# Two exponentials given ahead of two feed-forward blocks, and a router task moved from tap 84 to tap 80

## The chip, the cores and the metric

The kernel runs on one core of a Trainium2 chip. Times are device microseconds of that core. The kernel before has a median of 1639.95 us over 3 runs (1638.41 to 1640.2).

## The reference, cut to what matters

The input is 8 images of 256 channels by 32 x 32 positions, in float32. Each image goes through a linear-attention block and a mixture of six feed-forward experts, both with a residual.

```python
x = x + conv_attention(layernorm_over_channels(x))
t = tokens(x)
t = t + ffn(layernorm(t))

def ffn(x):
    logits = x.mean(axis=1) @ router_w.T
    probs = softmax(logits)
    vals, idx = top_k(probs, 2)
    vals = vals / vals.sum()
    ew = einsum(vals, partition_table[idx])
    ew = where(ew > 1e-6, ew, 0)
    h = gelu(x @ W1[e] + b1[e])
    out_e = h @ W2[e] + b2[e]
    return sum over e of ew[e] * out_e
```

The expert weights `ew` of an image depend on the mean over its tokens. There is one set of six weights per image; all experts are computed for all images. The attention block holds a 1 x 1 convolution to 768 channels (q, k and v), a depthwise 5 x 5 convolution of these, a grouped 1 x 1 convolution (the aggregation) and linear attention with 8 channels per head.

## The kernel before, in words

An image is kept as two tiles of 128 channels by 1024 positions. The layers with large matmuls split float32 values into a high and a low float16 part and add three products.

The order of all work is one list, `ORDER`, that `schedule()` (lines 81 to 269) writes. Every engine walks through this list and issues its own share of each item, in the order of the list. An engine waits by semaphores only, so what stands behind a waiting instruction on its engine waits too. Round `j` of the list works on the attention of image `j`, closes the attention of image `j - 1` (called `new`) and fills the room between with feed-forward blocks. A block (`ffn`) is 128 hidden units of 512 tokens; an image has 32 of them (two halves of the tokens, 16 blocks each).

`fill(k)` (lines 113 to 123) gives up to `k` blocks. With each it gives three things: the block's own first-layer matmuls and gelu (`ffn`); the expert-weight scaling and the splitting of earlier blocks whose image has its exponentials given (`gsplit`); and the second-layer matmuls (`second`) of the block four places back. Blocks 0 and 1 of an image may be given before its exponentials are given (line 115), its scalings may not (line 118). Behind the last block of a half a `final` evicts the sum.

The items around the change, with what each engine does:

- `logits`: two matmuls on TensorE (line 649), and an eviction of 11 numbers on ScalarE (line 818).
- the max task on VectorE (`max_task`, lines 1018 to 1026), which finds the largest logits and gives their negative as a bias.
- `exp` on ScalarE (lines 753 to 757): two small exponentials, of all logits and of the two largest. They need the max task. Exponential and gelu need different function tables, so a table load stands ahead of each when the other was last.
- the router task on VectorE (`route_task` and `ew_task`, lines 1028 to 1065): 14 small instructions in a chain. They need both exponentials. The last one writes `ewg`, the expert weights times a scale.
- `ffn`: six matmuls (line 533) into one of two PSUM banks `wbk`, and a gelu on ScalarE (line 825), which frees the bank.
- `gsplit`: two scalings on ScalarE (lines 730 and 731) that read `ewg`, and a subtraction on GpSimd (line 960).
- `second`: six matmuls (line 546) into the accumulator `acc`. The first block of a half waits until `final` has evicted the half before (line 544; the eviction is line 764).
- `agg`: the aggregation, four pieces of matmuls (line 584) for `k`, each into a bank `wbk` and evicted by ScalarE (line 790).
- `squares` on ScalarE (line 744), `sums` on GpSimd (lines 867 and 869), `stats` on TensorE (line 635), `rnorm` on GpSimd (line 883) and `rbc` on TensorE (line 644), evicted by ScalarE (line 816): the normalisation of a later image.
- `base`: some taps of the depthwise convolution of the next image, scaled on ScalarE (lines 700 and 705) and added on GpSimd (lines 924 and 930).

The two banks `wbk` are shared by all matmuls but `second`: a piece may start when the piece two places before it in the list has been evicted (lines 560 to 562).

VectorE does the other taps of the depthwise convolution, line 1113 for the most part, 138 instructions an image in three pairs of tiles (132 for image 0). Its small tasks are placed by their count of taps: the table `OF_LAST` (line 1077) puts tasks of the image before ahead of a given tap of this image. With 46 taps to a pair, taps 76 to 91 belong to the second pair. Behind the last image no taps are left, and the tasks follow each other.

Of the kernel before, what the change touches and what calls it, by code (L numbers as in the profile page):

```python
# [64 lines left out]
def base_taps(s, m):  # L65

    return (0 if m in (2, 3) else len(BASE_TAPS)) if s == 0 else 3
# [8 lines left out]
def tap_ops(s):  # L76

    return [(pair, tap, m) for pair in PAIRS for tap in tap_order(s, pair) for m in (2 * pair, 2 * pair + 1)]


def schedule():

    o = []
    given = set()
    waiting = []
    stream = [(s, f) for s in range(B) for f in range(NCH * FT)]
    todo = list(stream)
    unsplit = []

    def give(*items, n=1):  # L90
        for it in items:
            o.append(it)
            given.add(it)
            if it[0] in BANKED and n > 1:
                base(n)

    def base(n):
        o.extend(waiting[:n])
        del waiting[:n]

    def rest():
        base(len(waiting))

    def add_base(s, a):
        waiting.extend(("base", s, m, i) for m in (a, a + 1) for i in range(base_taps(s, m)))

    def second(k):
        s, n = stream[k]
        give(("second", s, n))
        if n % FT == FT - 1:  # L110
            give(("final", s, n // FT))

    def fill(k):
        for _ in range(k):
            if todo and ("low", todo[0][0], 1, CT - 1) in given and (("exp", todo[0][0]) in given or todo[0][1] < 2):
                i = len(stream) - len(todo)
                give(("ffn",) + todo.pop(0))
                while unsplit and ("exp", unsplit[0][0]) in given:
                    give(("gsplit",) + unsplit.pop(0))
                unsplit.append(stream[i])  # L120
                if i >= LAG:
                    second(i - LAG)
            base(1)

    def left(s):
        return sum(it[0] == s for it in todo)

    def qkv(s, m):
        return [("qkv", s, m, ch) for ch in range(NCH)]

    def agg(s, m):
        return [("agg", s, m, ch) for ch in range(NCH)]

    def norm_in(s):

        return [[("squares", s, 0, 0)], [("squares", s, 0, 1), ("sums", s, 0)],
                [], [("stats", s, 0), ("rnorm", s, 0)], [], [],
                [("rbc", s, 0, 0), ("rbc", s, 0, 1)], [("apply", s, 0, 0)], [("apply", s, 0, 1)]]

    def norm_out(s):  # L140

        return [[("high", s, 0, 0)], [("low", s, 0, 0), ("high", s, 0, 1)], [("low", s, 0, 1)]]

    give(("squares", 0, 0, 0), ("squares", 0, 0, 1), ("sums", 0, 0), ("weights", 0), ("stats", 0, 0), ("rnorm", 0, 0), ("rbc", 0, 0, 0), ("rbc", 0, 0, 1), ("apply", 0, 0, 0),
         ("apply", 0, 0, 1), ("weights", 1), ("high", 0, 0, 0), ("low", 0, 0, 0), ("high", 0, 0, 1), ("low", 0, 0, 1))
    give(*[it for m in range(2, QT) for it in qkv(0, m)])
    add_base(0, 2)
    add_base(0, 4)

    for j in range(B + 1):  # L150
        d, c, a, f = j < B, j >= 1, j + 1 < B, j + 2 < B
        new, nxt = j - 1, j + 1
        n = 3 if j == 0 else 1
        if c:
            give(*agg(new, 0), *agg(new, 1))
            fill(1)
            for t in range(TT):
                give(("att", new, 1, t))
                if t in (2, 5):
                    fill(1)  # L160
                if t == 3:
                    give(("scale", new, 1, 0))
            give(("scale", new, 1, 1))
        if j == 0:
            for group in norm_in(1)[:2]:
                give(*group)
        if d:
            give(*qkv(j, 0), *qkv(j, 1), n=n)
            add_base(j, 0)
            if j == 0:  # L170
                for group in norm_in(1)[2:]:
                    give(*group, n=n)
        out = norm_out(nxt) if a else [[], [], []]
        toks = [("tok", j, t) for t in range(TT)] if d else []
        if c:
            fill(1)
            give(("back", new, 1, 0, 0), ("back", new, 1, 0, 1))
            fill(1)
            give(("back", new, 1, 1, 0), ("back", new, 1, 1, 1))
            fill(1)  # L180
            give(("proj", new, 0, 0), *out[0], *toks[:2])
            give(("proj", new, 0, 1), *toks[2:4])
            give(("proj", new, 1, 0), *out[1], *toks[4:6])
            give(("proj", new, 1, 1), *toks[6:])
        else:
            give(*out[0], *out[1])
        if c:
            give(*out[2])
            fill(1 if d else 2)
            give(("squares", new, 1, 0), ("squares", new, 1, 1), ("sums", new, 1))  # L190
        else:
            give(*out[2], *toks, n=n)
        if d:
            give(("relu_q", j, 0))
            give(("kv", j, 0, 0), ("kv", j, 0, 1), n=n)
            give(("mask", j, 0), ("relu_q", j, 1))
        if c:
            fill(1)
            give(("stats", new, 1), ("rnorm", new, 1))
            fill(1)  # L200
        if d:
            give(*[("att", j, 0, t) for t in range(4)], n=n)
        if c:
            fill(1 if d else 2)
            give(("rbc", new, 1, 0), ("rbc", new, 1, 1), ("apply", new, 1, 0), ("apply", new, 1, 1))
        if d:
            give(("scale", j, 0, 0))
            give(*[("att", j, 0, t) for t in range(4, TT)], n=n)
        if c:
            give(("high", new, 1, 0))  # L210
            fill(1 if d else 2)
            give(("high", new, 1, 1))
        if d:
            give(("scale", j, 0, 1))
        if c:
            give(("low", new, 1, 0), ("low", new, 1, 1))
            if a:
                give(*qkv(nxt, 2))
        if d:
            give(*[("back", j, 0, ch, g) for ch in range(NCH) for g in range(2)], n=n)  # L220
        if c:
            give(("logits", new))
            if a:
                give(*qkv(nxt, 3))
            else:
                fill(1)
            fill(left(new - 1) + 2)
            give(("exp", new))
        rest() if j == 0 else None
        if d:  # L230
            give(*agg(j, 2), *agg(j, 3))
            if a and c:
                add_base(nxt, 2)
        if j == 0:
            give(*qkv(1, 2), *qkv(1, 3))
            add_base(1, 2)
        if d:
            for group in norm_in(j + 2) if f else [[]] * 5:
                give(*group)
                fill(1)  # L240
            fill(1)
            give(*agg(j, 4))
            fill(1)
            give(*agg(j, 5))
            fill(1)
            if a:
                for m in (4, 5):
                    for it in qkv(nxt, m):
                        give(it)
                        fill(1)  # L250
                add_base(nxt, 4)
            else:
                fill(4)
            give(("kv", j, 1, 0))
            fill(2)
            give(("kv", j, 1, 1))
            fill(1)
            give(("mask", j, 1))
            while left(new) > KEEP and new >= 0:
                fill(1)  # L260
            if j == 0:
                rest()
    k = len(stream)
    fill(k)
    rest()
    give(("gsplit",) + stream[-1])
    for i in range(k - LAG, k):
        second(i)
    return o
# [46 lines left out]
def build(nc, x, w_qkv, w_dw, w_pw, w_proj, bn, bn_rows, w_router, w1, b1, w2, b2, parts, out):  # L316
    with ExitStack() as ctx:
# [3 lines left out]
        def sem(name):  # L321
            return ctx.enter_context(nc.semaphore(name))
# [109 lines left out]
        route = sem("route")  # L432
# [532 lines left out]
        def _(dve):  # L965
# [108 lines left out]
                    ew_task(s, s % 2)  # L1074


            OF_LAST = {16: ("rden", 1, 0), 21: ("rden", 1, 1), 76: ("max",), 84: ("route",)}
            OF_THIS = {62: ("rden", 0, 0), 68: ("rden", 0, 1)}
            OF_FIRST = {92: ("rden", 0, 0), 98: ("rden", 0, 1)}

            for s in range(B + 1):
                if s == B:
                    for n in sorted(OF_LAST):
                        small_task(OF_LAST[n], s - 1)
                    continue
                for n, (pair, tap, m) in enumerate(tap_ops(s)):
                    if n in OF_LAST and s > 0:
                        small_task(OF_LAST[n], s - 1)
                    if n in (OF_FIRST if s == 0 else OF_THIS):
# [87 lines left out]
```

## Time and profile before

| what | value |
|---|---|
| median of 3 runs | 1639.95 us (1638.41 to 1640.2) |
| the profiled execution's own time | 1641.19 us |
| its span (first to last instruction) | 1639.5 us |
| mean granted TensorE clock | 0.935 of full |
| busy: TensorE matmul, VectorE, ScalarE, GpSimd | 83%, 78%, 65%, 59% of the span |
| chain that ended last, by engine | TensorE 46%, VectorE 20%, ScalarE 17%, GpSimd 8%, issue 8% |

In rows, PE is TensorE, PEld its weight loads, DVE VectorE, ACT ScalarE, POOL GpSimd. L730 is line 730 of the kernel. A row of the timeline has the start, the length of the merged instructions, engine, line, operation, out<-in, shapes and the count; in brackets stands the idle time of the engine ahead of it and what ended that. "hb" is the tile of gelu outputs, "gh" and "gl" its scaled high and low parts, "dacc" the depthwise accumulator, "kt" the transposed k, "sv" and "st" statistics of a normalisation, "tapb" and "dwo" the base taps. The granted clock is 1.00 at 2.4 GHz and 0.50 at 1.2 GHz. An image is 184 to 185 us behind the one before, for images 1 to 5.

### The profile page before, as it was taken

What the parts mean: (1) busy time and instruction counts of PE and PEld (TensorE: products, weight loads), DVE (VectorE), ACT (ScalarE), POOL (GpSimd) and SP (SyncE); (2) the same over time, 40 slices, a digit from 0 to 9 for tenths busy, and PEclk for the clock granted to TensorE, in tenths of its full rate; (3) what the DMA queues carried; (4) which work ended last, traced back from release to release, by engine and by line L of the source; (5) the groups of instructions that cost most, each with busy time, mean ns of one, the idle gap of its engine ahead of it and who ended that gap; (6) DMA issues with size and microseconds to landing.
All of it is one profiled execution on the core that took longest, in us unless ns stands there. A gap on an engine that the chain in (4) does not pass through costs nothing.

```text
span 1639.5 us, 18712 instructions
## 1 busy us (share of the span) xinstructions
PE 1362.3 (83%) x6844; PEld 786.6 (48%) x6844; DVE 1279.8 (78%) x1305; ACT 1063.9 (65%) x1855; POOL 973.1 (59%) x746
## 2 busy tenths in 40 slices
PE   5513678799888988899888988899888997999598
PEld 3313545455455445555465445555464545554343
DVE  3999989997979886996979886996969997970000
ACT  3534464767667766767667766777667865775476
POOL 3583556566559547666559547666566647344544
PEclk7767799899999999899999999899999998999899
DMA  5200000000001000000001000000001000100000
GB/s 182 77 0 26 0 27 1 1 27 13 1 1 65 13 1 1 32 33 14 1 1 63 16 1 1 24 16 13 1 1 39 13 1 1 39 13 1 0 14 26
DMA packets 14251, 32.75 MB, mean 20 GB/s; under 512 B 2384, under 2 KB 5328, under 8 KB 13904
## 3 DMA queue, kind: packets, MB, share of 16 engines
q1 hardware_dynamic: 14160, 31.56, 5.4%
q8 instruction: 54, 0.88, 0.2%
q14 instruction: 37, 0.30, 0.1%
HBM read 23.17 MB, written 8.39 MB: 19 GB/s over the span
## 4 chain that ended last, share of the span: by engine, by line
PE 46%; DVE 20%; ACT 17%; POOL 8%; issue 8%; DMA 1%; POOLq 0%; SPq 0%; ACTq 0%; DVEq 0%
PE wbk L533 20%; DVE dacc L1113 17%; PE acc L546 10%; PE wbk L625 6%; ACT gh L730 4%; ACT hb L731 3%; ACT tapb L705 2%; PE wbk L584 2%; POOL dwo L930 2%; PE wbk L635 2%; POOL gl L960 2%; PE wbk L579 1%; ACT dwo L700 1%; PE wbk L611 1%; ACT sum_b L810 1%
## 5 line engine op out<-in xcount | busy, mean ns | idle before, releaser
L1113 DVE SCALAR_TENSOR_TENSOR dacc<-qkvs,dww,dacc 128x930 f32<-128x930 f32 (+4 forms) x954 | 1053.2, 1189 | 0.0
L960 POOL TENSOR_TENSOR gl<-hb,gh 128x512 f16<-128x512 f32 x256 | 303.7, 1188 | 421.8 <-ACT hb L731 421.0
L825 ACT ACTIVATE hb<-wbk,b1s 128x512 f32<-128x512 f32 x256 | 175.5, 685 | 156.4 <-PE wbk L533 156.3
L930 POOL TENSOR_TENSOR dwo<-dwo,tapb 128x992 f32<-128x992 f32 (+1 forms) x104 | 240.2, 2309 | 13.4 <-ACT tapb L705 10.2
L546 PE MATMUL acc<-gh,w2h 128*128 128x512 f16 x512 | 197.0, 385 | 33.5 <-ACT sum_b L764 29.3
L546 PE MATMUL acc<-gh,w2l 128*128 128x512 f16 x512 | 197.8, 386 | 0.0
L546 PE MATMUL acc<-gl,w2h 128*128 128x512 f16 x512 | 197.7, 386 | 0.0
L730 ACT ACTIVATE gh<-hb,ewg 128x512 f16<-128x512 f32 x256 | 182.5, 713 | 9.6 <-DVE ewg L1065 9.6
L533 PE MATMUL wbk<-th,w1h 128*128 128x512 f16 x512 | 154.9, 385 | 33.5 <-ACT qr L807 16.7
L731 ACT ACTIVATE hb<-hb,ewg 128x512 f32<-128x512 f32 x256 | 182.3, 712 | 0.0
L1016 DVE RECIPROCAL den<-den 128x128 f32<-128x128 f32 x32 | 30.4, 949 | 176.7 <-ACT den L804 176.7
L533 PE MATMUL wbk<-tl,w1h 128*128 128x512 f16 x512 | 154.3, 383 | 0.0
L533 PE MATMUL wbk<-th,w1l 128*128 128x512 f16 x512 | 153.6, 382 | 0.0
L705 ACT ACTIVATE tapb<-qkvs,dww 128x1024 f32<-128x1024 f32 x104 | 118.5, 1145 | 24.0 <-POOL dwo L930 20.5
L781 ACT ACTIVATE qkvs<-wbk 128x512 f32<-128x512 f32 x96 | 56.5, 595 | 73.0 <-PE wbk L533 73.0
L546 PEld LDWEIGHTS acc<-gh,w2h 128*128 128x128 f16 x512 | 50.6, 99 | 99.5 <-issue 35.6
L611 PE MATMUL wbk<-kvm,qr 128*128 128x144 f32 x512 | 80.4, 296 | 18.3 <-ACT den L804 12.9
L948 POOL TENSOR_TENSOR yr<-yr,sum_b 128x512 f32<-128x512 f32 x32 | 41.6, 1299 | 87.2 <-ACT sum_b L810 86.4
L910 POOL TENSOR_TENSOR kt<-kt,den 128x1024 f32<-128x1024 f32 x32 | 63.6, 1997 | 45.8 <-DVE den L1016 45.8
L1105 DVE SCALAR_TENSOR_TENSOR dacc<-qkvs,dww,dwo 128x1024 f32<-128x1024 f32 x46 | 88.0, 1957 | 0.0
L533 PEld LDWEIGHTS wbk<-th,w1h 128*128 128x128 f16 x512 | 45.9, 98 | 83.6 <-ACT qr L807 20.0
L611 PEld LDWEIGHTS wbk<-kvm,qr 128*128 128x128 f32 x512 | 69.1, 189 | 32.7 <-ACT den L804 21.9
(146 smaller groups left out, 2236.1 us busy)
## 6 DMA issues: line engine op xcount, KB each, us to landing
xa<-x SPq DMA_DIRECT2D x8, 1024.0 KB, 5.0
yr<-x SPq DMA_DIRECT2D x8, 1024.0 KB, 5.0
out<-yr SPq DMA_DIRECT2D x16, 512.0 KB, 2.8
dwo<-w SPq DMA_DIRECT2D x1, 2048.0 KB, 11.0
yr<-w SPq DMA_DIRECT2D x2, 1024.0 KB, 16.6
dwo<-w_qkv SPq DMA_DIRECT2D x1, 768.0 KB, 4.4
wp<-w_proj SPq DMA_DIRECT2D x1, 512.0 KB, 12.6
pw<-w_pw SPq DMA_DIRECT2D x16, 24.0 KB
```

The lines of the kernel that those rows point to most:

```text
L533: last = nc.tensor.matmul(dst, w[:, k, m * P:(m + 1) * P], d[:, k, c * CH:(c + 1) * CH], start=(i == 0), stop=(i == len(parts) - 1))
L546: last = nc.tensor.matmul(acc[:, m, :], w[:, t, m * P:(m + 1) * P], d[:, f % GB, :], start=(t == 0 and i == 0), stop=(t == FT - 1 and i == 2),
L611: last = nc.tensor.matmul(b[:, g * RD:(g + 1) * RD], qr[:, g, t * P:(t + 1) * P], kvm[:, g, :], start=True, stop=True)
L625: last = nc.tensor.matmul(b[:], wp[:, k, m * P:(m + 1) * P], (ac, qr)[k // CT][:, k % CT, c * CH:(c + 1) * CH], start=(k == 0), stop=(k == ...
L705: ins = nc.scalar.activation(tapb[:, i % 2, :], qkvs[:, m, :], ACT.Copy, scale=w)
L730: nc.scalar.activation(gh[:, f % GB, :], hb[:, f % GB, :], ACT.Copy, scale=w).then_inc(g_high, 1)
L731: nc.scalar.activation(hb[:, f % GB, :], hb[:, f % GB, :], ACT.Copy, scale=w).then_inc(g_scaled, 1)
L825: last = nc.scalar.activation(hb[:, f % GB, :], b[:], ACT.Gelu, bias=b1s[:, f % FT:f % FT + 1], scale=1.0 / (X_SCALE * W_SCALE))
L930: ins = nc.gpsimd.tensor_tensor(d3[:, oy, ox], d3[:, oy, ox], t3[:, iy, ix], ALU.add)
L960: nc.gpsimd.tensor_tensor(gl[:, f % GB, :], hb[:, f % GB, :], gh[:, f % GB, :], ALU.subtract).then_inc(g_low, 1)
L1105: ins = nc.vector.scalar_tensor_tensor(out=dacc[:, m % 2, :], in0=qkvs[:, m, :], scalar=w, in1=dwo[:, m, :], op0=ALU.mult, op1=ALU.add)
L1113: ins = nc.vector.scalar_tensor_tensor(out=dst[:, oy, ox], in0=i3[:, jy, jx], scalar=dww[:, m, tap:tap + 1], in1=a3[:, oy, ox], op0=ALU.mu ...
```

## The change

The item `exp` is given ahead of the fill that gives the new image's blocks, in place of behind it. By the rule of `fill` block 1's place in the list is then followed by the scaling of block 0, since the exponentials are given by then. In round 7, where no next qkv pieces are left, one block is given ahead of `exp`, and the fill then gives one block more ahead of the aggregation than before. On VectorE the router task stands ahead of tap 80 in place of tap 84.

```diff
@@ -224,8 +224,8 @@
                 give(*qkv(nxt, 3))
             else:
                 fill(1)
+            give(("exp", new))
             fill(left(new - 1) + 2)
-            give(("exp", new))
         rest() if j == 0 else None
         if d:
             give(*agg(j, 2), *agg(j, 3))
@@ -1074,7 +1074,7 @@
-            OF_LAST = {16: ("rden", 1, 0), 21: ("rden", 1, 1), 76: ("max",), 84: ("route",)}
+            OF_LAST = {16: ("rden", 1, 0), 21: ("rden", 1, 1), 76: ("max",), 80: ("route",)}
             OF_THIS = {62: ("rden", 0, 0), 68: ("rden", 0, 1)}
             OF_FIRST = {92: ("rden", 0, 0), 98: ("rden", 0, 1)}
```

The list for image 1 (round 2), before and after. ("gsplit", 0, 31) belongs to the last block of image 0:

```
before: logits 1, qkv(3,3) x2, ffn 1.0, gsplit 0.31, second 0.28, ffn 1.1, second 0.29, exp 1,
        agg(2,2) x2, agg(2,3) x2, squares 4, ffn 1.2, gsplit 1.0, gsplit 1.1, second 0.30, base, squares 4
after:  logits 1, qkv(3,3) x2, exp 1, ffn 1.0, gsplit 0.31, second 0.28, ffn 1.1, gsplit 1.0, second 0.29,
        agg(2,2) x2, agg(2,3) x2, squares 4, ffn 1.2, gsplit 1.1, second 0.30, base, squares 4
```

## Rows read from the trace of the kernel before

**Rows 1.** Chain of waits from 440 to 680 us: start, length, what.

```profile
451.25 3.57 PE wbk L635 x32
...
498.25 2.72 PE acc L546 x6
500.97 4.88 PE wbk L635 x32
```

**Rows 2.** Timeline of VectorE, image 1, and the taps behind image 6's max task.

```profile
479.02 8.84 DVE L1113 SCALAR_TENSOR_TENSOR dacc<-qkvs,dww,dacc 128x930 f32<-128x930 f32 x8
487.77 0.16 DVE L1031 RECIPROCAL rt<-rt 128x1 f32<-128x1 f32 x1
...
491.00 0.18 DVE L1065 TENSOR_SCALAR ewg<-ew 128x22 f32<-128x22 f32 x1
...
1394.06 8.84 DVE L1113 SCALAR_TENSOR_TENSOR dacc<-qkvs,dww,dacc 128x930 f32<-128x930 f32 x8
```

**Rows 3.** Timeline of ScalarE, image 1.

```profile
476.88 0.60 ACT L781 ACTIVATE qkvs<-wbk 128x512 f32<-128x512 f32 x1 [0.70 <-PE wbk L533]
...
481.47 1.28 ACT L755 ACT_TABLE_LOAD   x1
...
483.26 1.19 ACT L790 ACTIVATE kt<-wbk 128x512 f32<-128x512 f32 x2
...
486.46 1.05 ACT L744 ACTIVATE nrm<-xa 128x1024 f32<-128x1024 f32 x1
...
488.83 0.69 ACT L825 ACTIVATE hb<-wbk,b1s 128x512 f32<-128x512 f32 x1
491.22 0.72 ACT L730 ACTIVATE gh<-hb,ewg 128x512 f16<-128x512 f32 x1 [1.70 <-DVE ewg L1065]
...
493.68 1.11 ACT L700 ACTIVATE dwo<-qkvs,dww 128x992 f32<-128x992 f32 x1
```

**Rows 4.** Table of waits, whole span: waited for, us in total, times, longest.

```profile
ACT gh L730 <- DVE ewg L1065: 9.6, 7, 2.1
```

**Rows 5.** Timeline of TensorE, images 1, 6 and 7.

```profile
481.86 4.07 PE L584 MATMUL wbk<-pw,dwo 128*128 128x128 f32 x32
...
498.25 0.59 PE L546 MATMUL acc<-gh,w2h 128*128 128x512 f16 x1 [5.84 <-ACT sum_b L764]
...
1411.33 0.42 PE L546 MATMUL acc<-gh,w2h 128*128 128x512 f16 x1 [2.67 <-ACT sum_b L764]
...
1554.52 0.38 PE L546 MATMUL acc<-gh,w2h 128*128 128x512 f16 x1 [3.41 <-ACT sum_b L764]
```

**Rows 6.** Windows of TensorE: stretch, length, busy (count), granted clock, DMA share, GB/s.

```profile
496.50:503.20 6.70, 4.95 (x18) 0.52 0.01 2
...
1411.30:1414.60 3.30, 3.27 (x9) 0.53 0.02 5
```

**Rows 7.** Timeline of GpSimd in image 1, and of ScalarE in image 3.

```profile
492.63 2.38 POOL L960 TENSOR_TENSOR gl<-hb,gh 128x512 f16<-128x512 f32 x2 [11.31 <-ACT hb L731]
...
883.87 1.15 ACT L705 ACTIVATE tapb<-qkvs,dww 128x1024 f32<-128x1024 f32 x1 [0.21 <-POOL dwo L924]
```

**Rows 8.** Timeline of ScalarE, the square roots at the start of the program.

```profile
13.28 1.28 ACT L678 ACT_TABLE_LOAD   x1
17.70 0.42 ACT L678 ACTIVATE qr<-qr 128x256 f32<-128x256 f32 x1 [3.14 <-DVE bnc L974]
```

**Rows 9.** Timeline of ScalarE, images 6 and 7.

```profile
1395.42 0.71 ACT L731 ACTIVATE hb<-hb,ewg 128x512 f32<-128x512 f32 x1
...
1541.37 0.71 ACT L731 ACTIVATE hb<-hb,ewg 128x512 f32<-128x512 f32 x1
...
1544.08 1.28 ACT L755 ACT_TABLE_LOAD   x1
...
1553.70 1.25 ACT L764 ACTIVATE sum_b<-acc,ob 128x512 f32<-128x512 f32 x2
```

**Rows 10.** Line 584's instructions: matmuls, ns min/median/max, first and last start us.

```profile
L584 PE MATMUL wbk<-pw,dwo x512: 272/275/583, 170.4 to 1428.1; 128*128 128x128 f32 x171
```

## The prediction

> **What bounds the kernel now.** I read the page's chain of work first: TensorE holds most of it, VectorE and ScalarE a fifth and a sixth, so no single engine sets the time and the stretch around the change decides. Images are numbered 0 to 7. I took the chain over one period of image 1 [rows 1]: it runs along VectorE's taps to the end of the router task, crosses to ScalarE's two expert-weight scalings, then to the eviction of the old image's sum, and only then to TensorE, where six second-layer matmuls start at 498.25 and need 2.72 us, followed by the norm statistics.
>
> The timeline of VectorE [rows 2] shows why: it never idles here. The eight taps 76 to 83 take 8.75 us (479.02 to 487.77), the router task starts at 487.77, and its last instruction, which gives `ewg`, ends at 491.18. ScalarE [rows 3] gives the exponentials at 481.47 (with a table load), evicts four aggregation tiles, squares, loads a table again, runs the gelu of block 2 and then waits 1.70 us for `ewg` at 491.22. In the table of waits this wait stands 7 times in 8 images, 9.6 us in all [rows 4]. TensorE has meanwhile run ahead and stands still for 5.84 us [rows 5], and its clock falls: 0.52 of full from 496.5 to 503.2 [rows 6], the lower level, 1.2 GHz.
>
> One more queue matters. GpSimd subtracts the low halves as soon as ScalarE has scaled them, from 492.63 in image 1, after 11.31 us of idleness, and then works without a pause through sums, statistics and base taps until ScalarE waits for its memset before a base tap and the evictions of the norm's broadcast (0.21 us of it in image 3) [rows 7]. I find the same wait in images 0 and 2 to 4, and a tie in image 1. So what moves the start of GpSimd's run moves the period.
>
> **The change, part by part.** *Nothing is added or removed.* The same exponentials and the same router task are issued, 8 times each; no DMA moves, and SP's queue is not passed. Moved are two exponentials with their table load on ScalarE, ahead of two gelus and one old scaling; and, by the rule in `fill`, the scaling of the new image's block 0, ahead of the four aggregation evictions, the squares and the gelu of block 2. GpSimd's subtraction of that block moves with it.
>
> *The exponentials* (image 1). The last qkv eviction ends at 477.48 [rows 3]. A table load runs ahead of the wait behind it: the square root's load ran at 13.28, its activation waited until 17.70 [rows 8]. So the load is over at 478.8, and the exponential starts when the max task has given its bias, just behind 479.02 [rows 2], say 479.15. Both take 0.5 us (481.47 plus 1.29 to 483.26, [rows 3]), the gelu's load 1.29, so the gelu of block 0 starts near 481.0. With it, the old scaling and the gelu of block 1 (0.6 + 1.23 + 0.7), ScalarE is free near 483.5. That is 2 to 3 us later than now, at no cost: the wait for `ewg`, next, lasts longer. The number of loads stays at two per image. A load takes 1.28 us [rows 3, 9], and behind the one at 481.47 both exponentials are done within 0.5 us more.
>
> The Trainium skill (ScalarE: Activation LUTs, What ACT_TABLE_LOAD costs) gives each switch a drain of some 1.38 us beside the 1.28 us. By that the two switches would cost 2.8 us more ahead of the wait, my estimate from that page's figure, which in image 1 would still be covered; no row here shows such a drain.
>
> *The router task.* Four taps earlier is 4 x 8.75/8 = 4.38 us [rows 2]: `ewg` is there at 486.84. VectorE's own sum is unchanged; taps 80 to 83 now come behind the task, still ahead of the end of the tap pair. It would wait if the exponentials were late: in image 1 they end at 479.7, tap 80 is due at 483.4. It is narrowest in image 6, whose order differs: scaling over at 1396.13, load and exponentials to 1398.0, against 1394.06 + 4.38 = 1398.4 [rows 2, 9]. No stall.
>
> *What is now queued behind the wait.* Before, from `ewg` to the end of the second scaling took 491.22 to 493.68, 2.46 us for two blocks [rows 3], 1.23 each. Now, from 486.84: block 0's scaling to 488.07; two evictions of 0.60, the first bank free at 488.67. TensorE has two banks, so its third aggregation starts only here; at 4.07 us for four [rows 5], about 0.9 to 1.0 each, the evictions of the third and fourth start at 489.7 and 490.6; the squares (1.05) from 491.1, the gelu of block 2 at 492.2, its scaling to 494.0. That is 7.2 us instead of 2.46, for a gain of 4.38: **plus 0.3 us**, at full clock.
>
> *The clock in the new gap.* TensorE finishes its second aggregation near 484.5 (its bank is the one of block 1's gelu) and starts the third at 488.7: 4.2 us idle, where it had none. In image 6, 2.67 us of idleness [rows 5] was enough for 0.53 [rows 6]. At the lower level the two aggregations left (0.9 each) and block 2's six matmuls (1.3, half of what six take at that level, [rows 1]) take 6.2 instead of 3.1 us; an aggregation matmul has 275 ns at the median and 583 at most [rows 10]. Block 2 then ends at 494.9 instead of under the squares at 492.2, so the second scaling is at most 2.7 us later: **plus 3.0 us**. The lower bound is plus 0.3. I take **plus 2.0**: a gap this long should lower the clock each time, but a part of the three pieces will lie outside the lower stretch.
>
> *What that makes.* GpSimd's long run begins with the second block's subtraction, so its end, and with it the period, moves by the same 2.0 us. The later stall of TensorE shrinks from 5.84 to some 1.3 us and its clock should hold, but TensorE waits there for GpSimd's work anyway; what is late next is the memset [rows 7]. Images 0, 1, 2, 3 and 5 have this pattern: 5 x 2.0 = **plus 10.0** (0.3 to 3.0 each). Image 4, the one without a wait [rows 4], gains of the four taps only what it needs: **0** (minus 0.7 to plus 1.0). In image 6 the fill now places block 2 ahead of the aggregations; the 1.7 us that the clock costs there (3.3 us at 0.53, [rows 6]) may be lost in the new gap instead: **0** (minus 1.7 to plus 0.9).
>
> *Image 7* has no taps. Its scaling ends at 1542.08, so the load starts 2.0 us earlier than at 1544.08 [rows 9], and VectorE answers at once. One gelu (0.6) comes behind the wait, so the eviction of the old sum moves from 1553.70 to 1552.3, **minus 1.4**, and TensorE, which waited 3.41 us there [rows 5] and sets the pace from there to the end, starts 1.4 earlier. If its clock holds over the shorter gap, another 1.7 us is saved; I take minus 2.2.
>
> Sum: 10.0 + 0 + 0 - 2.2 = plus 7.8 us. The profiled execution took 1641.2 us, 1.2 above the median; against the median 1639.95 that is **1647.7 us**.
>
> **The rivals.** *The clock holds* (0.17). If the new gap, broken by one aggregation, leaves the clock up, five images cost 0.3 each, image 4 gives 0.7, image 6 1.7 and image 7 2.2 to 3.1: minus 3.4, **1636.5**. For it: the old 5.84 us gap would be gone. Against: 2.67 us sufficed. It decides where the idleness ahead of the third aggregation comes below what lowered the clock.
>
> *GpSimd is not the gate* (0.13), **faster**. Then TensorE's regained clock counts: its second-layer matmuls start 2 us later (500.3), but need 1.3 and 3.6 us (the statistics' row at 451.25) instead of 2.72 and 4.88 [rows 1], ending at 505.2 instead of 505.85. Five times minus 0.6, image 7's minus 2.2: minus 5.2, **1634.8**. The point is the memset: it holds ScalarE by only 0.21 us [rows 7]; if GpSimd's subtractions run faster away from VectorE, the gate opens. Against: the wait recurs in four images.
>
> *Half of it* (0.12): the clock falls in half of the five gaps, plus 3.5, **1643.5**, on the line of what a measurement can tell.
>
> *The exponentials come late* (0.05): in image 6 the margin is 0.4 us, and in others it shrinks if qkv runs at the lower clock. A VectorE stall of 1 to 2 us in three images adds 4: **1652**.
>
> *A dearer switch* (0.03): a load that held the engine longer than its row would eat the cover in images 2 to 4 and half of image 7's gain, plus 3 on top: **1651**. The rows of loads [rows 3] speak against it. The drain that the Trainium skill (ScalarE: Activation LUTs, What ACT_TABLE_LOAD costs) states would do it. That the change does not take effect at all I exclude: the order of issue is fixed in the list.
>
> **How the numbers follow.** The forecast has 0.50. About 0.2% (3.3 us) is what a measurement of this kernel can tell from no change. Slower: 0.50 + 0.05 + 0.03 + 0.05 of *half of it* = 0.63. Faster: 0.08 of the first rival, on the line, and 0.09 of the second = 0.17. The rest, 0.20, is within. The forecast's own range is 1642 to 1653.5 (2.0 per image to 0.9 and to 3.0); with the cases on the other side 1636 to 1653.5.
>
> **What would show it.** Right: exponentials just behind the max task; ScalarE's wait for `ewg` grown to over 3 us in images 1 to 3; TensorE idle 3 to 5 us ahead of the third aggregation, with the clock at its lower level there and full in the stall before the norm statistics; GpSimd's second subtraction some 2 us later. Wrong: full clock over the aggregations, the broadcast's evictions not behind GpSimd's memset, or VectorE idle ahead of the router task.

## The result, and the profile after

The changed kernel is slower: 1661.22 us median (1658.65 to 1662.84, 4 runs) against 1640.08 us (1638.41 to 1645.49, 4 runs) for the kernel before, a ratio of 1.0122 with a 95% interval of 1.0095 to 1.0148. The forecast was 1647.7 us, plus 7.8. The sign was right; the size, plus 21, lies outside the range of 1636.0 to 1653.5. The profiled execution took 1661.43 us (span 1659.7), at a mean granted clock of 0.929 where it was 0.935.

I give every image a cost: the time from the eviction of its logits to the next image's (for image 7 to the end), after less before. In image 1 that is (666.37 - 477.89) - (659.39 - 474.24) = 3.33 us. The shift of the second scaling is measured in the same way, from the image's own logits. All such figures, here and below, come from one profiled execution of each kernel.

| image | forecast | cost after | second scaling later by |
|---|---|---|---|
| 0 | +2.0 | +3.44 | 3.02 |
| 1 | +2.0 | +3.33 | 2.60 |
| 2 | +2.0 | +3.09 | 2.59 |
| 3 | +2.0 | +3.41 | 2.80 |
| 4 | 0 | +2.85 | 1.82 |
| 5 | +2.0 | +4.35 | 2.03 |
| 6 | 0 | +2.68 | (other order) |
| 7 | -2.2 | -3.11 | -1.42 |
| sum | +7.8 | +20.0 | |

ScalarE in the kernel before, the timeline of image 1 where the section ahead of the prediction does not show it:

```profile
474.24 0.18 ACT L818 ACTIVATE lg<-wbk 128x11 f32<-128x11 f32 x1 [0.21 <-PE wbk L649]
...
505.89 0.18 ACT L813 ACTIVATE st<-wbk 128x16 f32<-128x16 f32 x1 [3.33 <-PE wbk L635]
...
515.76 1.06 ACT L816 ACTIVATE rb<-wbk 128x512 f32<-128x512 f32 x2
517.90 0.69 ACT L825 ACTIVATE hb<-wbk,b1s 128x512 f32<-128x512 f32 x1 [1.07 <-PE wbk L533]
...
659.39 0.18 ACT L818 ACTIVATE lg<-wbk 128x11 f32<-128x11 f32 x1 [0.26 <-PE wbk L649]
```

ScalarE in the changed kernel, timeline of image 1, which answers to [rows 3]:

```profile
477.89 0.18 ACT L818 ACTIVATE lg<-wbk 128x11 f32<-128x11 f32 x1 [0.21 <-PE wbk L649]
...
481.15 1.28 ACT L755 ACT_TABLE_LOAD   x1
482.80 0.30 ACT L755 ACTIVATE ex<-lg,rt 128x11 f32<-128x11 f32 x1 [0.37 <-DVE rt L1026]
...
483.40 1.28 ACT L825 ACT_TABLE_LOAD   x1
484.70 0.69 ACT L825 ACTIVATE hb<-wbk,b1s 128x512 f32<-128x512 f32 x1
...
490.81 0.72 ACT L730 ACTIVATE gh<-hb,ewg 128x512 f16<-128x512 f32 x1 [3.62 <-DVE ewg L1065]
...
494.78 0.60 ACT L790 ACTIVATE kt<-wbk 128x512 f32<-128x512 f32 x1 [1.68 <-PE wbk L584]
496.49 0.60 ACT L790 ACTIVATE kt<-wbk 128x512 f32<-128x512 f32 x1 [1.11 <-PE wbk L584]
...
499.94 1.11 ACT L700 ACTIVATE dwo<-qkvs,dww 128x992 f32<-128x992 f32 x1
...
509.57 0.18 ACT L813 ACTIVATE st<-wbk 128x16 f32<-128x16 f32 x1 [0.76 <-PE wbk L635]
...
520.95 1.15 ACT L705 ACTIVATE tapb<-qkvs,dww 128x1024 f32<-128x1024 f32 x1 [0.81 <-POOL dwo L924]
522.01 0.58 ACT L816 ACTIVATE rb<-wbk 128x512 f32<-128x512 f32 x1
...
524.96 0.69 ACT L825 ACTIVATE hb<-wbk,b1s 128x512 f32<-128x512 f32 x1 [1.62 <-PE wbk L533]
...
666.37 0.18 ACT L818 ACTIVATE lg<-wbk 128x11 f32<-128x11 f32 x1 [0.26 <-PE wbk L649]
```

Image 1 comes in 3.65 us late (477.89 against 474.24). The steps behind it, as shifts against before: the second scaling ends, and the base tap starts, 6.26 late (499.94 against 493.68, [rows 3]); the statistics are evicted only 3.68 late (509.57 against 505.89), so TensorE and ScalarE have all of it back; the first eviction of the norm's broadcast is again 6.25 late (522.01 against 515.76), behind GpSimd's memset; and the gelu behind it 7.06 late (524.96 against 517.90). So 2.6 us come from the wait and the clock behind it, and another 0.8 us at the broadcast, which no step of the forecast has.

TensorE in the changed kernel, timeline of images 1, 5 and 7; these rows answer to [rows 5]:

```profile
485.51 1.08 PE L584 MATMUL wbk<-pw,dwo 128*128 128x128 f32 x8
487.24 1.16 PE L584 MATMUL wbk<-pw,dwo 128*128 128x128 f32 x8 [0.64 <-ACT hb L825]
492.67 3.78 PE L584 MATMUL wbk<-pw,dwo 128*128 128x128 f32 x16 [4.28 <-ACT kt L790]
504.51 0.38 PE L546 MATMUL acc<-gh,w2h 128*128 128x512 f16 x1 [1.24 <-ACT sum_b L764]
505.80 1.95 PE L635 MATMUL wbk<-mean_w,rb 128*128 128x128 f32 x16
...
519.88 2.83 PE L644 MATMUL wbk<-spread,sv 128*128 128x128 f32 x16 [2.58 <-POOL sv L883]
...
1267.03 1.16 PE L584 MATMUL wbk<-pw,dwo 128*128 128x128 f32 x8 [1.66 <-ACT hb L825]
1269.78 1.04 PE L533 MATMUL wbk<-th,w1h 128*128 128x512 f16 x2 [1.59 <-ACT vt L792]
...
1576.45 0.38 PE L546 MATMUL acc<-gh,w2h 128*128 128x512 f16 x1 [1.60 <-ACT sum_b L764]
```

Windows of TensorE after (stretch, length, busy, granted clock, DMA share, GB/s), around the third aggregation, the old stall, the broadcast, and in image 5:

```profile
492.70:496.10 3.40, 3.40 (x16) 0.50 0.00 0
...
503.30:515.00 11.70, 10.49 (x65) 1.00 0.12 47
...
519.90:526.00 6.10, 6.10 (x28) 0.72 0.01 1
...
1269.70:1277.00 7.30, 7.22 (x29) 0.62 0.00 0
```

The same view of the kernel before, at the broadcast:

```profile
517.00:526.00 9.00, 9.00 (x43) 1.00 0.01 3
```

In the changed kernel the clock stands at its lower level over the third and fourth aggregation (0.50), is full again at the old stall (1.00, against 0.52 in [rows 6]), and falls a second time behind a 2.58 us wait for GpSimd's `sv`. GpSimd in the changed kernel, timeline of image 1, answering to [rows 7]:

```profile
486.68 1.15 POOL L960 TENSOR_TENSOR gl<-hb,gh 128x512 f16<-128x512 f32 x1 [6.71 <-ACT hb L731]
492.22 1.16 POOL L960 TENSOR_TENSOR gl<-hb,gh 128x512 f16<-128x512 f32 x1 [4.38 <-ACT hb L731]
500.11 1.16 POOL L960 TENSOR_TENSOR gl<-hb,gh 128x512 f16<-128x512 f32 x1 [6.74 <-ACT hb L731]
...
518.08 1.66 POOL L883 TENSOR_TENSOR sv<-sv,mhalf 128x8 f32<-128x8 f32 x1
...
520.80 0.12 POOL L924 MEMSET dwo<- 128x32 f32 x1
```

From 500.11 on it pauses for no more than 0.20 us until `sv`. In the kernel before the memset stood 6.26 us earlier:

```profile
514.54 0.12 POOL L924 MEMSET dwo<- 128x32 f32 x1
```

The table of waits shows the wait for `ewg` in all 8 images, and more than twice as long in all as in [rows 4]:

```profile
ACT gh L730 <- DVE ewg L1065: 21.7, 8, 4.0
```

### The profile page after: what moved, and what is told of

Read it like the earlier page. It is cut to its first block, busy times and chain, and to the rows that moved or that the text cites. A ratio compares the mean times of both kernels' runs of the same rounds, so it can differ in the third digit from the quotient of the medians.

```text
span 1659.7 us, 18711 instructions
## 1 busy us (share of the span) xinstructions
PE 1373.5 (83%) x6844; PEld 798.0 (48%) x6844; DVE 1287.3 (78%) x1305; ACT 1060.6 (64%) x1854; POOL 974.8 (59%) x746
## 4 chain that ended last, share of the span: by engine, by line
PE 48%; DVE 18%; ACT 18%; POOL 8%; issue 7%; DMA 1%; POOLq 0%; SPq 0%; ACTq 0%; DVEq 0%
PE wbk L533 20%; DVE dacc L1113 15%; PE acc L546 10%; PE wbk L625 6%; ACT gh L730 4%; ACT hb L731 4%; PE wbk L584 4%; ACT tapb L705 2%; PE wbk L635 2%; POOL dwo L930 2%; PE wbk L644 2%; PE wbk L579 1%; ACT dwo L700 1%; ACT hb L825 1%; PE wbk L599 1%
## 5 line engine op out<-in xcount | busy, mean ns | idle before, releaser
L584 PE MATMUL wbk<-pw,dwo 128*128 128x128 f32 x512 | 78.5, 315 | 30.0 <-ACT kt L790 22.6
L584 PEld LDWEIGHTS wbk<-pw,dwo 128*128 128x128 f32 x512 | 74.9, 227 | 36.7 <-ACT kt L790 23.9
L1105 DVE SCALAR_TENSOR_TENSOR dacc<-qkvs,dww,dwo 128x1024 f32<-128x1024 f32 x46 | 92.5, 2054 | 0.0
```

The lines of the kernel that those rows point to most:

```text
L584: last = nc.tensor.matmul(b[:, i * P:(i + 1) * P], dwo[:, m, o:o + P], pw[:, m, :], start=True, stop=True)
L1105: ins = nc.vector.scalar_tensor_tensor(out=dacc[:, m % 2, :], in0=qkvs[:, m, :], scalar=w, in1=dwo[:, m, :], op0=ALU.mult, op1=ALU.add)
```

## The experiments

In the expectations T is the forecast's mechanism: block 0's scaling now stands ahead of the aggregation evictions, so the wait for `ewg` stops TensorE, and its clock falls. The other letters stand for what each text sets against it. Image costs are reckoned as in the table.

**The two halves of the change.** A gives the exponentials early and leaves the router task at tap 84:

```diff
-  76: ("max",), 80: ("route",)}
+  76: ("max",), 84: ("route",)}
```

> One part alone: the exponentials (and with them block 0's scaling) given early, the router task left at tap 84. Theory T (what costs is the scaling ahead of the aggregation evictions: all of these now stand behind the wait for ewg, and GpSimd's run and the period move with it): ewg is 4.4 us later than in the changed kernel, so six images lose another 4 us each: 1685 to 1690 us, ScalarE's wait for ewg near 8 us an image, TensorE's gap ahead of the third aggregation near 8 us. Rival R (it is the router task at tap 80 that costs, by VectorE's order): as the kernel before, 1636 to 1642 us.

Measured: 1675.28 us, ratio 1.0218 (1.0200 to 1.0237), slower than the change itself. The wait for `ewg` grew to 48.3 us in all (8 times, 8.4 at most), and TensorE's gap ahead of the third aggregation to 6.45 us in image 1:

```profile
494.37 3.78 PE L584 MATMUL wbk<-pw,dwo 128*128 128x128 f32 x16 [6.45 <-ACT kt L790]
```

So the harm is in the order of the list and not in the router task's place. The time is 10 us below T's range: four taps are 4.4 us for each of seven images, but images 0 to 6 cost 4.1 to 6.5 us, only 0.5 to 3.8 more than with the change. A part of what they save is the second stall at the broadcast: in images 1 to 4 of A the wait for `sv` is 0.6 to 0.8 us, and the clock holds.

B leaves the exponentials where they were and moves the router task alone (the edit of the diff's last line in the kernel before).

> The other part alone: the router task at tap 80, the list as before. T: nothing new stands behind the wait; ewg comes up to 4.4 us earlier, less what VectorE waits for exponentials that are given late (none in images 0 and 1, about 1.2 us in 2, 3 and 6, 2.7 in 4), so ScalarE's waits of 9.6 us in all nearly vanish and 5 to 8 us are gained: 1632 to 1635 us. R: slower than before, near 1655 to 1661 us.

Measured: 1637.51 us, ratio 0.9985 (0.9973 to 0.9998). The sign is T's, but the gain, 0.15%, is far from the 5 to 8 us of T: VectorE now waits for the exponentials. Image 7's wait (9.4 us, 9.6 before) is an old one; new are 11.3 us in six waits, in images 1 to 6. In image 1, where T had expected none, 2.58 us stand ahead of the first instruction of the router task:

```profile
485.66 0.16 DVE L1031 RECIPROCAL rt<-rt 128x1 f32<-128x1 f32 x1 [2.58 <-ACT rt L757]
```

The exponentials ended 10.9 us behind the logits there, against 9.1 in the kernel before; TensorE's clock over the 4.5 us behind these logits was 0.61, against 1.00.

**The order alone.** C has both parts of the change, but block 0's scaling stays in its old place, behind block 2's gelu, since `fill` learns of the exponentials only after it has given its blocks:

```diff
-            give(("exp", new))
+            o.append(("exp", new))
             fill(left(new - 1) + 2)
+            given.add(("exp", new))
```

> Both parts of the change, but block 0's scaling back in its old place behind the aggregation evictions, the squares and block 2 (the list is told of the exponentials only behind the fill). T: the cover is back: no wait for ewg in images 0 to 6, no TensorE gap ahead of the third aggregation, one table load less on the path; the second scaling ends 2 to 2.6 us earlier than in the kernel before in images 0 to 6, 1.5 to 2 in image 7: 1622 to 1630 us. R: still 1655 to 1661 us. Third theory U (the exponentials' place costs, by gelus held back 3 us): 1645 us or more.

Measured: 1626.95 us (1624.94 to 1627.21), ratio 0.9918 (0.9899 to 0.9936), faster than both kernels. C's list is that of the kernel before with nothing moved but the item `exp`, two blocks earlier (one in images 6 and 7). Against the changed kernel block 0's scaling and its subtraction are back in their place, and in image 6 block 2 stands behind the aggregations again. 1.0122 less 0.9918 is 2.0%, some 33 us; the profiles put 4.9 of it in image 6. ScalarE of image 1 in C (lines from 229 on are one higher):

```profile
481.61 0.59 ACT L791 ACTIVATE kt<-wbk 128x512 f32<-128x512 f32 x1
...
486.25 0.68 ACT L826 ACTIVATE hb<-wbk,b1s 128x512 f32<-128x512 f32 x1
486.82 0.72 ACT L731 ACTIVATE gh<-hb,ewg 128x512 f16<-128x512 f32 x1
```

No wait for `ewg`: it is over at 484.85, under the evictions and the squares. Only image 7 keeps 0.5 us of it. The images cost -2.38, -2.53, -1.36, -0.36, -0.95, -1.10, -2.23 and -3.68 us. The second scaling ends 2.1 to 3.0 us earlier in images 0 to 2, as T has it or more, but only 0.3 to 1.9 in images 3 to 6.

J is C with the router task at tap 84.

> Exponentials early and block 0's scaling in its old place, but the router task back at tap 84. T: ewg comes where it came before, 4 us later than ScalarE could use it, so ScalarE waits 2 to 3 us in images 0 to 6 and most of the gain of the kernel with the scaling put back is lost: 1635 to 1641 us (image 7 keeps its 2 us). If the gain there came from the table loads alone: 1627 us again.

Measured: 1635.74 us, ratio 0.9973 (0.9957 to 0.9990), in T's range. The wait for `ewg` is back, 14.1 us in 8 waits: 2.5 to 2.9 us in images 0 to 2, as T has it, and 0.2 to 2.0 in images 3 to 6. So the four taps are worth 0.55% in this order, and 0.15% (B) where the exponentials are late.

**The clock.** D puts work that changes nothing into TensorE's new gap: 16 matmuls of a zero tile into `acc` ahead of the wait for the third aggregation's bank in images 1 to 4, and 9 in image 5. (The lines that make the zero tile are left out here.)

```diff
+                if it[0] == "agg" and it[2:] == (3, 0) and 2 <= s < B - 1:
+                    for i in range(16 if s < 6 else 9):
+                        nc.tensor.matmul(acc[:, i % CT, :], zero[:], w1h[:, 0, 0:CH], start=False, stop=False,
+                                         skip_group_check=True)
```

> The changed kernel with matmuls of a zero tile (16 ahead of the third aggregation's wait in images 1 to 4, 9 in image 5), which add nothing to the sums and keep TensorE busy over most of the gap. T with the clock as the price: the granted clock stays 1.00 over the third and fourth aggregation and block 2, the second scaling of images 1 to 5 ends 1.5 to 2 us earlier, TensorE's later wait for GpSimd's statistics shrinks below 1 us and its second fall of the clock goes too: 10 to 13 us less than the changed kernel, 1648 to 1651 us. If the queue alone is the price and the clock costs nothing: 1659 to 1663 us.

Measured: 1652.38 us, ratio 1.0066 (1.0042 to 1.0091), a little above T's range. The gap and the aggregation behind it in image 1, and the windows of D:

```profile
489.90 3.62 PE L563 MATMUL acc<-w1h,zero 128*128 128x512 f16 x16
494.35 2.05 PE L589 MATMUL wbk<-pw,dwo 128*128 128x128 f32 x16 [0.83 <-ACT kt L795]
...
519.64 3.41 PE L649 MATMUL wbk<-spread,sv 128*128 128x128 f32 x16 [2.60 <-POOL sv L889]
```

```profile
484.00:515.00 31.00, 28.16 (x160) 1.00 0.05 18
515.00:526.00 11.00, 8.40 (x41) 0.84 0.30 96
```

The aggregation takes 2.05 us in place of 3.78, and the second scaling of image 1 is 0.66 us late in place of 2.60: of the 2.6 us, 1.9 are the clock and 0.7 the queue. Images 4 and 5 go from 1.82 and 2.03 to 0.32 and 0.82. In images 2 and 3 the zero matmuls outlast the gap: the third aggregation starts 1.10 and 1.29 us after its bank is free, and the shift shrinks less, from 2.59 and 2.80 to 1.37 and 2.01. But the broadcast still waits 2.6 us for `sv`, a wait that T had expected to shrink below 1 us, and in images 1 to 3 its clock still falls; in image 4 it holds behind the same wait.

H adds 9 of the same matmuls ahead of the broadcast's wait in images 1 to 4 (condition `it[0] == "rbc" and it[2:] == (0, 0) and 4 <= s < B`).

> The filler kernel with a second filler, 9 matmuls of the zero tile ahead of TensorE's wait for GpSimd's statistics in images 1 to 4. T: the second fall of the clock goes, so the broadcast's 16 matmuls need 1.8 to 2 us instead of 2.8 to 3.4 and the next block 1.3: 0.8 us an image, some 3 us less than with one filler, 1648 to 1650 us, and the image's cost is the delay of its second scaling alone. If the second fall costs nothing: 1651 to 1654 us as with one filler.

Measured: 1649.06 us, ratio 1.0063 (1.0040 to 1.0086). In its profile the broadcast takes 2.02 us, and images 1 to 4 cost 0.95, 0.80, 1.43 and 0.38 us, where D had 1.45, 2.14, 2.55 and 0.63:

```profile
515.28 2.11 PE L567 MATMUL acc<-w1h,zero 128*128 128x512 f16 x9
518.04 2.02 PE L653 MATMUL wbk<-spread,sv 128*128 128x128 f32 x16 [0.65 <-POOL sv L893]
```

The medians of D and H can't be told apart; that the second fall costs is read from the profiles, image by image. Between the second scaling and that of block 7, images 1 to 4 lose 0.81, 0.73, 0.75 and 0.75 us in the changed kernel, 0.50, 0.74, 0.78 and 0.02 in D, and 0.00 to 0.03 in H.

**GpSimd as the gate.** F is the kernel before and G the changed kernel, both with one addition of GpSimd's run ahead of the statistics cut to 64 of its 1024 columns (the norm of images 3 to 7, which runs in the periods of images 0 to 4); the variance of these norms is left out but for those columns.

```diff
-                nc.gpsimd.tensor_tensor(nrm[:, 0, :], nrm[:, 0, :], nrm[:, 1, :], ALU.add)
+                n = 64 if L == 0 and s >= 3 else T
+                nc.gpsimd.tensor_tensor(nrm[:, 0, 0:n], nrm[:, 0, 0:n], nrm[:, 1, 0:n], ALU.add)
```

> The kernel before with 2.2 us less on GpSimd in each of images 0 to 4: the second sum ahead of the norm statistics adds 64 of 1024 columns (this part of the computation is left out). T (there GpSimd and ScalarE arrive at the base tap within 0.9 us of each other, so a shorter GpSimd run is worth only that): 0 to 3 us less, 1636 to 1640 us. If GpSimd alone is the gate there: 8 to 11 us less, 1628 to 1632 us.

> The changed kernel with the same part left out (64 of 1024 columns in the second sum of images 0 to 4). T (in the changed kernel GpSimd's late run is the gate, and TensorE's wait for its statistics lowers the clock a second time): the wait of 2.6 us ahead of the broadcast shrinks below 1 us, the clock holds there, and 2 to 3 us go in each of the five images: 1646 to 1651 us. If TensorE's or ScalarE's own work is the gate, GpSimd's cut is worth nothing: 1659 to 1663 us.

Measured: F 1641.25 us, ratio 1.0006 (0.9991 to 1.0020); G 1647.79 us, ratio 1.0057 (1.0037 to 1.0077). In the kernel before the shorter run of GpSimd gains nothing at the median, where 8 to 11 us were due if GpSimd alone were the gate. (In F's profile images 0 to 4 cost 1.7 us less in all, inside T's 0 to 3; image 6, which the cut doesn't touch, costs 2.93 more.) In the changed kernel the cut gains 0.65%, 11 us. The broadcast of image 1 in G no longer waits long, and its clock holds:

```profile
513.69 2.02 PE L644 MATMUL wbk<-spread,sv 128*128 128x128 f32 x16 [0.56 <-POOL sv L884]
```

G's profile is of its fastest execution (1640.0 us), so I take no image costs from it.

**The images left.** K has H's zero matmuls, and 8 more ahead of the second aggregation in images 0, 5 and 6, 16 ahead of image 0's third, and 8 ahead of block 2 of image 5. The part of the edit that L changes:

```diff
+                if it in (("agg", 1, 2, 1), ("agg", 6, 2, 1), ("agg", 7, 2, 1), ("ffn", 5, 2)):
+                    for i in range(8):
+                        nc.tensor.matmul(acc[:, i % CT, :], zero[:], w1h[:, 0, 0:CH], start=s == 1, stop=s == 1,
+                                         skip_group_check=True)
```

> The changed kernel with the zero matmuls of both runs before and with more of them: 8 ahead of the second aggregation in images 0, 5 and 6, 16 ahead of the third in image 0, and 8 ahead of block 2's first layer in image 5. They put off no work that TensorE has to do, they fill its gaps. T, that the excess of images 0, 5 and 6 over the queue's few tenths is TensorE's clock as in images 1 to 4: image 0 costs 1 to 2 us in place of 3.4, image 5 about 1 in place of 3.3, image 6 minus 1.7 to minus 0.3, so some 4 us less than with fillers in images 1 to 4 alone: 1643 to 1647. R, that images 0 and 5 pay for the order of the queue itself: no change, 1648 to 1650.

Measured: 1649.92 us, ratio 1.0052 (1.0035 to 1.0069). The total lies where R had it. Image 0 costs 1.72 us in place of 3.44, as T has it; image 6 costs 0.09 in place of 2.68, above T's bound of -0.3. Image 5 went the other way, 4.68: the zero matmuls ahead of block 2 ran until 1239.1 where its bank was free at 1237.2, so they did hold back work, and the clock then fell at the aggregation for `v`, to 0.50 from 1260 to 1266. L takes those of images 5 and 6 out and puts 7 ahead of image 5's second piece for `v` and 7 ahead of the block behind it.

```diff
-                if it in (("agg", 1, 2, 1), ("agg", 6, 2, 1), ("agg", 7, 2, 1), ("ffn", 5, 2)):
-                    for i in range(8):
+                if it in (("agg", 1, 2, 1), ("agg", 6, 4, 1), ("ffn", 5, 8)):
+                    for i in range(7):
```

> The run before with the zero matmuls of images 5 and 6 taken out again (those ahead of block 2 held it back by 1.9 us in image 5) and 7 put instead ahead of image 5's second aggregation for v and 7 ahead of the block behind it, where the clock fell to 0.50 in a pair of gaps of 1.66 and 1.59 us. Image 0 keeps its own, 7 in place of 8 ahead of the second aggregation. T, that image 5's excess is that second fall: image 5 costs 0 to 1.3 us in place of 3.3 to 4.7, image 0 stays at 1.2 to 2.2: 1643 to 1647. R, that the price of image 5 is the queue behind the wait: image 5 stays above 2.5, 1647 to 1650.

Measured: 1646.39 us, ratio 1.0056 (1.0041 to 1.0071). Image 0 costs 1.48, image 6, bare again, 2.69, image 5 2.35. The total lies in T's range, and image 5 between T and R. Two rows of image 5 in L:

```profile
1231.03 3.04 PE L597 MATMUL wbk<-pw,dwo 128*128 128x128 f32 x16 [2.34 <-ACT kt L803]
...
1256.30 0.60 PE L534 MATMUL wbk<-th,w1h 128*128 128x512 f16 x2
```

The first matmul behind the aggregation for `v` takes 0.60 us in place of 1.04, and nothing is lost there any more; but a gap of 2.34 us was left ahead of the third aggregation, the clock fell there, and the second scaling is 2.75 late. In H, where zero matmuls left a gap of 0.95 us and these 16 matmuls took 2.05 us, it was 0.74 late. `ewg` came 0.35 us later in L than in H, so by far the most of both of image 5's losses is falls of the clock. By the ratios D, H, K and L can't be told apart.

## Why the prediction was right in direction and wrong in size

**Right.** *The exponentials at no cost*: in image 1 the load ran from 481.15, ahead of the wait, and the exponential 0.03 us behind the max task. *The router task 4.38 us earlier*, in part: counted from the image's logits, `ewg` came 4.4 us earlier in images 0 and 6, but 3.5 to 4.2 in images 1 to 5. *The queue behind the wait* and *the clock in the new gap*: TensorE's idleness ahead of the third aggregation was 4.28 us (4.2 forecast), at 0.50 behind it, and ScalarE's wait over 3 us in images 1 to 3. D shows the two as causes, not company. *Image 7*: the second-layer matmul came 1.42 us earlier (1576.45 less 1554.52 less the 23.35 by which the image came in; minus 1.4 forecast). The clock then held, 1.00 from 1575 to 1581, where it was 0.72 from 1554 to 1560 before; so it took all of the 1.7 us of which I took half: -3.1, the end of its own bounds.

**The step that failed** is *what that makes*, in three places.

1. "I take plus 2.0" for images 0, 1, 2, 3 and 5. The second scaling was 2.0 to 3.0 us late, 2.75 in the mean of images 0 to 3. That is 3 us of the error. The queue was sized rightly: from the end of `ewg` to the end of the second scaling D, at full clock, takes 7.33 us in images 1 and 4, which is 4.73 more than the 2.60 of image 1 before (7.2 less 2.46 in the forecast). The clock's price was 1.5 to 1.9 us in images 1 to 3 (8.8 to 9.3 less 7.33), about the 1.7 in my 2.0. What was short there was the gain of the four taps: `ewg` came only 4.06, 3.64 and 3.47 us earlier and not 4.38, most of it because the router task itself took 3.78 to 4.16 us where it took 3.41 before (see the last section). In image 0, where `ewg` did come 4.45 us earlier, the clock cost more: 10.07 us for the same stretch, against 7.70 in L.
2. "Its clock should hold, but TensorE waits there for GpSimd's work anyway." The clock did hold in the old stall, and this made TensorE early at the next meeting with GpSimd. A wait that before did not stand out (six of the broadcast's matmuls took 0.83 us at full clock, and 517 to 526 stood at 1.00) became 2.58 us, the clock fell a second time, and the 16 matmuls took 2.83 us and not 2.0. It cost 0.8 us in image 1 (7.06 less 6.25), and 0.7 to 0.8 in images 2 to 4. In image 5, which has no norm, it came at the aggregation for `v` (gaps of 1.66 and 1.59 us, 0.62 behind them), for some 2.7 us between the scalings of blocks 6 and 8. I had asked what is late next; I had not asked whether the one that waits for it would be cold.
3. "Image 4: 0" and "image 6: 0". Image 4 had no wait for `ewg` before, but with the scaling ahead of the evictions it has one, 3.17 us, and TensorE a gap of 3.82: it belonged with the five, and the four taps did not make up for the order. In image 6 the gain that I set against the new gap did come, but the gap cost more. With a bare gap of 1.99 us ahead of the second aggregation and 0.50 over the third and fourth, block 2's second scaling was 3.1 us late, where my sum had 1.7; two blocks later 1.7 of it was back, and 1.4 stayed. How much of the work lies at the lower level is not fixed by the gap alone: behind a bare gap of 2.02 us in H the mean clock was 0.60 over the same two aggregations, and the scaling 1.4 late, and in K, with the gap filled and the clock at 1.00, 0.2. The last 1.3 us came at the image's end, at the broadcast of the next norm. There TensorE waits for `sv` equally long in both kernels, but behind the wait the clock held in the kernel before and fell in the changed one:

```profile
1525.74 2.02 PE L644 MATMUL wbk<-spread,sv 128*128 128x128 f32 x16 [3.07 <-POOL sv L883]
```

```profile
1547.82 3.30 PE L644 MATMUL wbk<-spread,sv 128*128 128x128 f32 x16 [3.06 <-POOL sv L883]
```

The first row is of the kernel before, the second of the changed one. All twelve profiles have this wait, 3.06 to 3.07 us; over the 3 us behind it the clock was 1.00 in the kernel before, D, G and H, and 0.50 to 0.74 in the other eight, F among them, which has the list of the kernel before. So nothing here shows that this part is the change's doing.

Together the three are 12 us: images 0 to 3 cost 5.3 more than forecast, image 4 2.9, image 5 2.4, image 6 2.7 (1.3 of it at its end), and image 7 0.9 less.

**The rivals.** *The clock holds* falls by the windows. *GpSimd is not the gate* falls by G and by the shifts of image 1: the statistics were back at 3.68, GpSimd's memset stood at 6.26 (520.80 against 514.54). *Half of it* falls: the clock fell in all five images, to 0.50 to 0.55 over the third and fourth aggregation. *The exponentials come late* falls for the change, where the router task never waits for them in images 0 to 6, and is what B pays. *A dearer switch* falls: the gelu's load ends at 484.68 and the gelu starts at 484.70. Each of the 16 loads ahead of an exponential or a gelu starts 0.02 us behind the activation before it, and the activation behind it starts within 0.02 us of its end, but for image 1's exponential, which waits 0.37 us for VectorE. The drain that the Trainium skill (ScalarE: Activation LUTs, What ACT_TABLE_LOAD costs) gives each switch is not to be seen here.

Every step of the forecast was reckoned against the kernel before, so it never asked what the change would be worth without its one bad order. C answers that: minus 13 us. The loss was the price of one scaling's place (in image 6 with that of block 2), some 33 us, on top of a gain.

## What to carry to other kernels

When an item moves ahead in a list that an in-order engine walks, look at what a rule of the list lets follow it, and at what then stands behind its wait: here a scaling that came along unasked held four evictions, and they held TensorE. Put the wait behind work that is ready without it, and an earlier producer pays (C); in front of it, it costs more than it brings. And where a matrix engine regains its clock in one place, follow it to the next engine it meets: it may arrive early, wait, and lose the clock again.

## What the runs showed that I had not expected

The router task itself took 3.78 us in image 1 (487.00 to 490.77) and up to 4.16 in images 2 to 5, where it took 3.41 before, though its instructions are the same; in images 0 and 6 it took 3.40. One small copy stretched, on VectorE after (timeline of image 1, and image 2 with another victim):

```profile
487.33 0.53 DVE L1036 CAST rt<-ix 128x2 f32<-128x2 uint32 x1
...
675.68 0.98 DVE L1040 TENSOR_SCALAR rt<-rt 128x2 f32<-128x2 f32 x1
```

Before they took 0.16 and 0.23 us. Both end just as GpSimd's subtraction ends (486.68 plus 1.15 is 487.83, against 487.86; 675.48 plus 1.15 is 676.63, against 676.66). The earlier router task had moved under a subtraction of GpSimd. The Trainium skill (GPSIMD Engine Reference, Specifications) says that GpSimd shares its SBUF interfaces with VectorE, and that it contends with VectorE's instructions in a 2-port perf mode or with two SBUF inputs. The trace fits a contention, at 0.4 and 0.75 us for these two; whether they are of those kinds no run here shows, and that the sharing is the cause was not tried.

The second surprise is that like gaps were not followed by like clocks. In image 5 a pair of gaps of 1.66 and 1.59 us was followed by the lower level in the changed kernel, in H and in K, where the first matmul behind them takes 1.03 to 1.04 us; in C the same two gaps stand, and that matmul takes 0.60 us. Between the scalings of blocks 6 and 8 image 5 lost 2.7 us in K and nothing in C. The wait of 3.06 us at the end of image 6 is another such case. What decides it stayed open.
